# Edge attention on one Trainium2 core: the gathered rows' buffer grows from eight to ten quarters, paid for with spilled tiles and one product buffer less

## The chip, the cores and the metric

The program runs on one core of one Trainium2 chip. The metric is the time of one execution in device microseconds, the median of several runs. The engines are PE (TensorE), DVE (VectorE), ACT (ScalarE), POOL (GpSimd) and SP, which here only issues DMAs.

## What is computed

A graph transformer layer over N = 3125 nodes of width 256 and E = 50000 edges. The part around the change is the attention over edges, whose destinations come sorted:

```
q, k, v = per node, 8 heads of 32
sim  = sum over d of q[dst] * k[src] / sqrt(32)      # per edge and head
p    = exp(sim - max of sim over the edges with this dst)
agg  = segment_sum(p * v[src], dst) / segment_sum(p, dst)
x    = x + agg @ Wo.T + bo + linear attention(x)
x    = x + mixture of 8 experts (layernorm(x))
```

## The kernel before

The layer runs as five blocks, one after the other, with all engines meeting between them: preparation (projections, edge tables), linear attention, edge attention, `finish` (output projection, routing) and `experts`. The change lies in `attention`.

Edge attention walks over CH = 28 chunks of U = 16 steps. A step is 128 edges, one per partition, that lie in one window of 125 destination nodes; the last chunk has only 8 real steps. For each step POOL issues one gather (L965): an indirect DMA that fetches, for 128 edges, a row of 520 words (the key and, per head, the value and a one) from `kv_d` in DRAM. Before each of them a small POOL copy (L955) makes an index column ready eight steps ahead. Four steps are a quarter ("quad"); a chunk has QUADS = 4 of them, so a quarter holds four gathers of 266 KB.

The rows lie in two tiles, `slot0` for even chunks and `slot1` for odd ones, so in eight quarters. A quarter is read twice by DVE: by `product` (L1058, query times key, as soon as the gathers of the quarter have landed: semaphore `arrived`) and, one to two rounds later, by `weigh` (L1074, weight times value, `pv_made`). A gather into a quarter therefore waits until the `weigh` of the same quarter two chunks earlier has been done (L963).

Engines run in rounds; round n works on three chunks at a time. The order on DVE in round n, with c = n - 1 and b = n - 2, is written out by hand: weigh(b,2), an add, product(n,0), an add, local maxima of c, reduce(n,0), carries of c, weigh(b,3), adds, maxima of c, product and reduce(n,1), weigh(c,0), product(n,2), reduce(n,2), rescale, weigh(c,1), adds, `turned_hots` (L1052) for chunk n+1, product and reduce(n,3). `turned_hots` reads `locrow`, which SP loads for each chunk with one 500 KB DMA (L941) as soon as the last `turned_hots` is over. PE spreads the queries (L1197) and sums the weighted values (L1207, which waits for `hot` of ACT, `pv` of DVE and the last add). ACT builds `hot` for a quarter (L992 four Abs, L996 one Relu).

POOL begins the block with 17 tiles of an addition (L648) and eight index copies, and then issues the gathers of chunks 2 to 27 without anything else between them; chunks 0 and 1 were gathered in the block before. `rounds` (L918) emits rounds 0 and 1, a loop of 12 passes over two rounds each, and four more rounds.

After the attention, `finish` multiplies with `woT` on PE (L1488) and adds the product to `base`, the residual tiles (L1385).

Of the kernel before, what the change touches and what calls it, by code (L numbers as in the profile page):

```python
# [25 lines left out]
H, HD = 8, 32  # L26
# [28 lines left out]
SOON = 8  # L55
EARLY = U * KV - NT * (2 * HID + 1)
assert EROWS * W2 >= E and EROWS % 2 == 0 and PAIRS % 2 == 0 and REST == U // 2 and CH % 2 == 0 and CAP == 489
# [83 lines left out]
def prepare(nc, m, io):  # L141
# [3 lines left out]
    with ExitStack() as ctx:  # L145
# [7 lines left out]
        qr = sb("q_rest", [TT, 2, D])  # L153
        qm = sb("qm", [TT, NT, MH])
        sq = sb("sq", [TT, 2, D])
# [49 lines left out]
        with nc.Block() as block:  # L205
# [114 lines left out]
            def _(dve):  # L320
# [37 lines left out]
                def rows_numbered():  # L358
# [5 lines left out]
                    st.then(dve.tensor_scalar(away[:, :], step_no[:, :], U - 0.5, float(NOBODY), ALU.is_ge, ALU.mult))  # L364
# [286 lines left out]
def linear_attention(nc, m, io):  # L651

    with ExitStack() as ctx:
# [19 lines left out]
        ysq = sb("ysq", [TT, 2, D])  # L673
# [187 lines left out]
def attention(nc, m):  # L861
# [7 lines left out]
    with ExitStack() as ctx:  # L869
# [5 lines left out]
        slot, locrow = [m.slot0, m.slot1], m.locrow  # L875
        hotT = sb("hotT", [TT, U, 128], BF16)
        prod = sb("prod", [128, 2, 4, D])
# [15 lines left out]
        habs = sb("habs", [128, 4, TT])  # L893
# [41 lines left out]
        with nc.Block() as block:  # L935
            @block.sync
            def _(sp):
                def body(n, par, turn):
                    if exists(n) and not (isinstance(n, int) and n == 0):
                        wait(sp, S.hotT_made, n)  # L940
                        sp.dma_start(locrow[:, :], loc_c[bass.ds(n, 1), :].to_broadcast([TT, U * 128])).then_inc(S.loc_in, 16)  # L941
                rounds(sp, body)

            @block.gpsimd
            def _(pool):
# [8 lines left out]
                def index(c, par, u):  # L954
                    pool.tensor_copy(m.idx[:, par, u:u + 1], at(m.src_e, c)[:, u:u + 1]).then_inc(S.idx_ready, 1)  # L955

                def gather(c, par, steps):
                    for u in range(steps):
                        if u % 4 == 0:
# [3 lines left out]
                            pool.wait_ge(S.pv_made, QUADS * c + u // 4 + 1 - 2 * QUADS)  # L963
                            pool.nop(nofuse=True)
                        pool.indirect_dma_start(slot[par][:, u, :], None, m.kv_d,  # L965
                                                bass.IndirectOffsetOnAxis(ap=m.idx[:, par, u:u + 1].bitcast(U32), axis=0),
                                                bounds_check=N - 1, oob_is_err=False).then_inc(S.arrived[par * QUADS + u // 4], 16)
                        if u + 8 < steps:
                            index(c, par, u + 8)
                        elif steps == U:  # L970
                            index(c + 1, 1 - par, u + 8 - U)
                for u in range(8):
                    index(2, 0, u)
                with pool.Fori(1, CH // 2 - 1) as k:
                    gather(2 * k, 0, U)
                    gather(2 * k + 1, 1, U)
                gather(CH - 2, 0, U)
                gather(CH - 1, 1, U - REST)

            @block.scalar  # L980
            def _(act):
# [6 lines left out]
                def hots(c, g):  # L988

                    wait(act, S.hot_made, QUADS * c + g)  # L990
                    for u in range(4 * g, 4 * g + 4):
                        last = act.activation(habs[:, u % 4, :], m.iota_w[:, :], ACT.Abs, bias=at(m.nloc_e, c)[:, u:u + 1])  # L992
                    last.then_inc(S.hot_abs, 1)
                    act.wait_ge(S.hot_abs, QUADS * c + g + 1)
                    wait(act, S.summed, PC * c + 2 * g - 2)
                    act.activation(hot[:, 4 * (g % 2):4 * (g % 2) + 4, :], habs[:, :, :], ACT.Relu, bias=m.one_col[:, 0:1],  # L996
# [24 lines left out]
                def body(n, par, turn):  # L1021
# [25 lines left out]
            def _(dve):  # L1047
# [6 lines left out]
                def product(n, par, turn, q):  # L1054
                    dve.wait_ge(S.arrived[par * QUADS + q], 64 * turn + 64)
                    dve.wait_ge(S.q_spread, QUADS * n + q + 1)
                    wait(dve, S.reduced, QUADS * n + q - 1)
# [812 lines left out]
```

## Time and profile before

| | |
|---|---|
| median of 3 runs | 1229.21 us (1227.22 to 1231.34) |
| the profiled execution, its own time | 1221.9 us |
| its span in the profile | 1220.2 us |
| DVE busy over the span | 71% |
| POOL busy over the span | 56% |
| PE busy over the span | 77% |
| the attention block | about 204 to 908.5 us |

The profile is that of one execution. Busy shares are means over blocks with different limits, so what is said on the attention is read from that block alone: from who waits for whom there, and from the timeline of single engines. In a timeline the number in brackets is how long the engine had been idle, and whose work ended that.

### The profile page before, as it was taken

How to read it: one execution, taken by the hardware profiler on the slowest of the kernel's cores; microseconds unless marked ns; L12 is line 12 of the kernel's file. 1: busy time of each engine (PE TensorE's matmuls, PEld its weight loads, DVE VectorE, ACT ScalarE, POOL GpSimd, SP SyncE). 2: the span in 40 equal slices, each digit the busy share in tenths (PEclk: the TensorE clock that was granted, in tenths of full speed). 3: DMA queues.
4: the chain of work that ended last, by engine and by line, in shares of the span. 5: the costliest groups of instructions: out<-in, count | busy, mean ns of one | idle time of the engine just before them, and what ended most of it. 6: DMA issues, size and time to landing. Idle time of an engine off the chain costs nothing. (4 is left out here: it accounts for less than half of the span.)

```text
span 1220.2 us, 18503 instructions
## 1 busy us (share of the span) xinstructions
PE 940.9 (77%) x4059; PEld 648.3 (53%) x4060; DVE 867.9 (71%) x1761; ACT 478.9 (39%) x1312; POOL 681.8 (56%) x1043
## 2 busy tenths in 40 slices
PE   4899776676777677787777768776768389999996
PEld 3455453454545455555555545554546246666664
DVE  3778767778888788887888788887968604444333
ACT  3556535434444344533444334443433033222330
POOL 2534276567778777787778877887500212222321
PEclk9999877878889877887788878888889779999998
DMA  4344272366566655566556655555413143233310
GB/s 146 103 103 95 79 225 77 89 175 191 164 175 184 179 166 164 170 175 179 153 169 163 173 153 163 154 158 161 116 46 109 63 142 124 90 111 102 137 59 8
DMA packets 79290, 164.39 MB, mean 135 GB/s; under 512 B 15472, under 2 KB 46963, under 8 KB 79251
## 3 DMA queue, kind: packets, MB, share of 16 engines
q0 software_dynamic: 38464, 110.26, 32.7%
q1 hardware_dynamic: 38883, 52.22, 13.3%
q10 hardware_dynamic: 1904, 1.45, 0.4%
q8 instruction: 16, 0.26, 0.1%
q14 instruction: 23, 0.19, 0.1%
HBM read 162.03 MB, written 17.65 MB: 147 GB/s over the span
## 5 line engine op out<-in xcount | busy, mean ns | idle before, releaser
L965 POOL DMA_INDIRECT slot<-kv_d,idx x408 | 426.6, 1046 | 149.3 <-DVE at_pv L1074 87.5
L1207 PE MATMUL at_pa<-at_pv,at_hot 128*125 128x264 f32 x880 | 288.5, 472 | 135.4 <-DVE agg L1088 133.3
L1207 PEld LDWEIGHTS at_pa<-at_pv,at_hot 128*125 128x125 f32 x880 | 186.7, 229 | 214.1 <-DVE agg L1088 140.2
L1197 PE MATMUL at_pq<-q,at_hotT 125*128 x1320 | 190.0, 306 | 11.1 <-POOL at_sign L951 7.0
L1058 DVE TENSOR_TENSOR at_prod<-at_pq,slot 128x1024 f32<-128x1024 f32 x110 | 134.0, 1218 | 76.6 <-DMA slot<-kv_d,idx 72.0
L1197 PEld LDWEIGHTS at_pq<-q,at_hotT 125*128 125x128 bf16 x1320 | 138.8, 109 | 46.0 <-issue 13.9
L1074 DVE TENSOR_TENSOR at_pv<-slot,at_pp 128x1056 f32<-128x1056 f32 x110 | 136.9, 1244 | 15.0 <-PE at_pp L1230 14.8
L992 ACT ACTIVATE at_habs<-iota_w,nloc_e 128x125 f32<-128x125 f32 x440 | 138.0, 384 | 3.4
L1065 DVE TENSOR_REDUCE at_sc<-at_prod 128x32 f32<-128x1024 f32 x110 | 133.4, 1213 | 2.0
L996 ACT ACTIVATE at_hot<-at_habs,one_col 128x500 f32<-128x500 f32 x110 | 78.3, 712 | 126.0 <-PE at_pa L1207 122.6
L1613 POOL DMA_INDIRECT out<-slot,node_s x32 | 31.9, 997 | 166.9 <-DVE slot L1645 166.0
L1680 PE MATMUL xp<-slot,hm 128*128 128x256 f32 (+1 forms) x512 | 113.1, 379 | 0.0
L1634 DVE TENSOR_TENSOR y<-xp,b 128x256 f32<-128x256 f32 (+1 forms) x32 | 13.6, 424 | 139.3 <-PE xp L1680 139.3
L1670 PE MATMUL xp<-hT,slot 128*128 128x489 f32 x256 | 108.6, 583 | 0.8 <-ACT hT L1578 0.8
L1680 PEld LDWEIGHTS xp<-slot,hm 128*128 128x128 f32 (+1 forms) x512 | 94.3, 185 | 18.2 <-issue 3.5
L1088 DVE TENSOR_TENSOR agg<-agg,at_pa 125x264 f32 x220 | 92.6, 421 | 7.6 <-PE at_pa L1207 2.8
L1027 ACT ACTIVATE at_row<-at_pchain 1x256 f32<-1x256 f32 x28 | 10.5, 376 | 202.9 <-PE at_pchain L1219 202.9
L1589 ACT ACTIVATE hm<-xp,b 128x489 f32<-128x489 f32 x64 | 42.9, 671 | 114.5 <-PE xp L1670 114.5
L955 POOL COPY idx<-src_e 128x1 int32 (+1 forms) x408 | 80.5, 198 | 2.6
L1670 PEld LDWEIGHTS xp<-hT,slot 128*128 128x128 f32 x256 | 49.5, 194 | 55.7 <-issue 49.9
L1224 PE MATMUL at_pchain<-at_one_c,at_line 1*128 1x1 f32 x112 | 25.0, 323 | 45.5 <-DVE at_line L1109 45.5
L629 PE MATMUL pa<-slot,xnT 128*125 128x512 f32 x100 | 51.7, 642 | 4.1 <-DVE vst L436 4.1
(316 smaller groups left out, 1263.7 us busy)
## 6 DMA issues: line engine op xcount, KB each, us to landing
slot<-in_w SPq DMA_DIRECT2D x16, 1024.0 KB, 6.3
locrow<-loc_d SPq DMA_DIRECT2D x28, 500.0 KB
slot<-kv_d,idx POOLq DMA_INDIRECT x408, 3.8
kv_d<-vst SPq DMA_DIRECT2D x25, 128.9 KB
base<-in_x SPq DMA_DIRECT2D x5, 625.0 KB
kv_d<-kst SPq DMA_DIRECT2D x25, 125.0 KB
row_d<-base SPq DMA_DIRECT2D x5, 625.0 KB
out<-base SPq DMA_DIRECT2D x1, 3125.0 KB
```

The lines of the kernel that those rows point to most:

```text
L955: pool.tensor_copy(m.idx[:, par, u:u + 1], at(m.src_e, c)[:, u:u + 1]).then_inc(S.idx_ready, 1)
L965: pool.indirect_dma_start(slot[par][:, u, :], None, m.kv_d, bass.IndirectOffsetOnAxis(ap=m.idx[:, par, u:u + 1].bitcast(U32), axis=0), bou ...
L992: last = act.activation(habs[:, u % 4, :], m.iota_w[:, :], ACT.Abs, bias=at(m.nloc_e, c)[:, u:u + 1])
L996: act.activation(hot[:, 4 * (g % 2):4 * (g % 2) + 4, :], habs[:, :, :], ACT.Relu, bias=m.one_col[:, 0:1], scale=-1.0).then_inc(S.hot_made, 1)
L1058: dve.tensor_tensor(prod[:, q % 2, :, :], pq[q % 2].rearrange("p (i d) -> p i d", i=4), slot[par][:, 4 * q:4 * q + 4, 0:D], ALU.mult).then ...
L1065: dve.tensor_reduce(sc[:, :, 4 * q:4 * q + 4].rearrange("p h i -> p i h"), prod[:, q % 2, :, :].rearrange("p i (h d) -> p i h d", h=H), X, ...
L1074: dve.tensor_tensor(pv[:, 4 * (q % 2):4 * (q % 2) + 4, :, :], slot[par][:, four, D:KV].rearrange("p i (h c) -> p i h c", h=H), spread(ph[: ...
L1088: dve.tensor_tensor(dst, dst, pa[p % 2][:, 0:H * VW].rearrange("p (h c) -> p h c", h=H), ALU.add).then_inc(S.added, 1)
L1197: mm = pe.matmul(pq[q % 2][:, u * D:(u + 1) * D], hotT[:, 4 * q + u, :], at(m.q3, wins[u // 2])[:, part, :], start=(part == 0), stop=(part ...
L1207: mm = pe.matmul(pa[p % 2][:, 0:H * VW], hot[:, u % 8, :], pv[:, u % 8, :, :].rearrange("p h c -> p (h c)"), start=(u % 2 == 0), stop=(u % ...
L1670: mm = pe.matmul(p1[f % 2][:, 0:CAP], w1[par][:, c, f * 128:(f + 1) * 128], hT[par][:, c, 0:CAP], start=(c == 0), stop=(c == 1))
L1680: mm = pe.matmul(p2[i % 2][0:sizes[i], 0:D], hm[:, f, 128 * i:128 * i + sizes[i]], w2[par][:, f, :], start=(f == 0), stop=(f == FC - 1))
```

## The change

The gathered rows lie in a ring of RING = 10 quarters. Quarter q of chunk c lies at place (4c + q) mod 10. Places 0 to 7 are the old tiles, place 8 is the room of the first eight residual tiles of `base`, place 9 is a new tile `extra`. A gather waits for the `weigh` ten quarters back instead of eight. Room comes from:

- SP writes the first eight tiles of `base` (1.02 MB) and `woT` (0.27 MB, which now lies in `extra`) to DRAM at the start of the attention, and loads both again once the last `weigh` is done; `finish` waits for both before its first use of them.
- `prod` has one buffer instead of two, so a product waits for the reduction just before it.
- `habs` is gone: ACT writes the Abs straight into `hot`, and so waits for PE's sums before the four Abs and not before the Relu.
- some tiles of other blocks (`q_rest`, `sq`, `ysq`, `hT`) move into `extra`.

Since 5 chunks are 20 quarters, two turns of the ring, the loop now holds five rounds: three rounds ahead of it, 4 passes over five rounds, seven rounds behind it.

```diff
-            body(0, 0, 0)
-            body(1, 1, 0)
-            with eng.Fori(1, CH // 2 - 1) as k:
-                body(2 * k, 0, k)
-                body(2 * k + 1, 1, k)
-            for n in range(CH - 2, CH + 2):
-                body(n, n % 2, n // 2)
+            for n in range(LOOP):
+                body(n, n, 0)
+            with eng.Fori(0, LOOPS) as k:
+                for s in range(LOOP, LOOP + TURN):
+                    body(TURN * k + s, s, k)
+            for n in range(CH - 5, CH + 2):
+                body(n, n, 0)
...
+                sp.dma_start(m.first_rows.rearrange("p (t d) -> p t d", t=SOON), m.base[:, 0:SOON, :]).then_inc(S.spilled, 16)
+                sp.dma_start(m.wo_d.rearrange("p (c n) -> p c n", c=2), m.woT[:, :, :]).then_inc(S.spilled, 16)
...
+                sp.wait_ge(S.pv_made, QUADS * (CH - 1) + quads(CH - 1))
+                sp.dma_start(m.woT[:, :, :], m.wo_d.rearrange("p (c n) -> p c n", c=2)).then_inc(S.reloaded, 16)
+                sp.dma_start(m.base[:, 0:SOON, :], m.first_rows.rearrange("p (t d) -> p t d", t=SOON)).then_inc(S.reloaded, 16)
...
-                            pool.wait_ge(S.pv_made, QUADS * c + u // 4 + 1 - 2 * QUADS)
+                            if s == 2 and q < 2:
+                                pool.wait_ge(S.spilled, 32)
+                            else:
+                                pool.wait_ge(S.pv_made, QUADS * c + q + 1 - RING)
...
-                    wait(act, S.hot_made, QUADS * c + g)
+                    four = slice(4 * (g % 2), 4 * (g % 2) + 4)
+                    wait(act, S.summed, PC * c + 2 * g - 2)
                     for u in range(4 * g, 4 * g + 4):
-                        last = act.activation(habs[:, u % 4, :], m.iota_w[:, :], ACT.Abs, bias=at(m.nloc_e, c)[:, u:u + 1])
+                        last = act.activation(hot[:, u % 8, :], m.iota_w[:, :], ACT.Abs, bias=at(m.nloc_e, c)[:, u:u + 1])
...
-                    wait(dve, S.reduced, QUADS * n + q - 1)
+                    wait(dve, S.reduced, QUADS * n + q)
...
+                    if t == 0:
+                        dve.wait_ge(S.reloaded, 32)
                     dve.tensor_tensor(m.base[:, t, :], m.base[:, t, :], po[par][:, 0:D], ALU.add).then_inc(S.x2_made, 1)
...
+                pe.wait_ge(S.reloaded, 32)
```

On POOL, at the start of the attention, this is the order before: the additions, the index copies, and then the first gather of chunk 2, already in the loop and behind a wait for a `weigh`.

```order
L648 TENSOR_TENSOR base<-base,agg 125x256 [waits y_scaled] x17
L955 COPY idx<-src_e 128x1 x8
L974 UNCONDITIONAL_BRANCH
L974 ISA
L963 ISA [waits idx_ready]
L965 DMA slot0<-kv_d,idx 128x520 [waits pv_made]
L955 ISA
L955 COPY idx<-src_e 128x1
```

And this is the same place in the changed kernel (`base` and `extra` are the places 8 and 9 of the ring).

```order
L651 TENSOR_TENSOR base<-base,agg 125x256 [waits y_scaled] x17
L971 COPY idx<-src_e 128x1 x8
L986 DMA base<-kv_d,idx 128x520 [waits idx_ready,spilled]
L971 COPY idx<-src_e 128x1
...
L986 DMA extra<-kv_d,idx 128x520 [waits idx_ready,spilled]
L971 COPY idx<-src_e 128x1
...
L986 DMA slot0<-kv_d,idx 128x520 [waits idx_ready,pv_made]
L971 COPY idx<-src_e 128x1
```

Eight gathers now wait for the spill alone, and the ninth is the first that waits for a `weigh`.

On SP, in the attention and at the start of `finish`, this stood before: one `locrow` DMA a round, and then the loads of `finish`.

```order
L941 DMA locrow<-loc_d 125x2048 [waits hotT_made]
L923 UNCONDITIONAL_BRANCH
...
L941 DMA locrow<-loc_d 125x2048 [waits hotT_made] x2
L935 UNCONDITIONAL_BRANCH
L1335 UNCONDITIONAL_BRANCH [waits barrier_Pool_Activation_PE_DVE_SP_release]
L1337 DMA gb<-in_gate_b 125x8
```

Now the spill stands ahead of the first `locrow`, and the reload behind the last (`first_rows_d` and `wo_d` are the new tensors in DRAM).

```order
L947 DMA first_rows_d<-base 125x2048
L948 DMA wo_d<-extra 128x528
L953 DMA locrow<-loc_d 125x2048 [waits hotT_made] x2
L924 UNCONDITIONAL_BRANCH
...
L953 DMA locrow<-loc_d 125x2048 [waits hotT_made] x5
L956 DMA extra<-wo_d 128x528 [waits pv_made]
L957 DMA base<-first_rows_d 125x2048
L944 UNCONDITIONAL_BRANCH
```

Two DMAs are queued ahead of the `locrow` of chunk 1 on SP's queue, and two ahead of the loads of `finish`.

## Rows read from the trace of the kernel before

**Rows 1.** The page's part 1, busy time, share of the span, instructions.

```profile
PE 940.9 (77%) x4059; PEld 648.3 (53%) x4060; DVE 867.9 (71%) x1761; ACT 478.9 (39%) x1312; POOL 681.8 (56%) x1043
```

**Rows 2.** The waits: engine, line, waited for: us in total, times, longest.

```profile
POOL slot L965 <- DVE at_pv L1074: 87.5, 62, 13.8
DVE at_prod L1058 <- DMA slot<-kv_d,idx: 72.0, 25, 5.6
POOL slot L965 <- issue: 57.3, 317, 1.6
...
DVE at_run L1106 <- ACT at_row L1027: 17.3, 18, 1.5
...
DVE at_pv L1074 <- PE at_pp L1230: 14.8, 16, 1.5
```

**Rows 3.** Timeline, POOL's gathers: start, us, instruction, idle before it.

```profile
231.64 1.08 POOL L965 DMA_INDIRECT slot<-kv_d,idx  x1 [13.78 <-DVE at_pv L1074]
...
414.34 1.02 POOL L965 DMA_INDIRECT slot<-kv_d,idx  x1 [1.58 <-issue]
...
588.83 1.02 POOL L965 DMA_INDIRECT slot<-kv_d,idx  x1 [0.42 <-issue]
...
592.96 1.36 POOL L965 DMA_INDIRECT slot<-kv_d,idx  x1 [0.15 <-issue]
...
874.43 1.00 POOL L965 DMA_INDIRECT slot<-kv_d,idx  x1 [0.30 <-issue]
```

**Rows 4.** Timeline of DVE: a table, first products of rounds, the last weigh.

```profile
215.97 1.02 DVE L1052 TENSOR_SCALAR at_hotT<-locrow,iota_p 125x2048 bf16<-125x2048 bf16 x1
...
245.47 1.22 DVE L1058 TENSOR_TENSOR at_prod<-at_pq,slot 128x1024 f32<-128x1024 f32 x1 [5.57 <-DMA slot<-kv_d,idx]
...
576.37 1.22 DVE L1058 TENSOR_TENSOR at_prod<-at_pq,slot 128x1024 f32<-128x1024 f32 x1 [2.53 <-DMA slot<-kv_d,idx]
...
600.74 1.22 DVE L1058 TENSOR_TENSOR at_prod<-at_pq,slot 128x1024 f32<-128x1024 f32 x1 [3.08 <-DMA slot<-kv_d,idx]
...
874.39 1.23 DVE L1058 TENSOR_TENSOR at_prod<-at_pq,slot 128x1024 f32<-128x1024 f32 x1 [0.22 <-issue]
...
903.47 1.25 DVE L1074 TENSOR_TENSOR at_pv<-slot,at_pp 128x1056 f32<-128x1056 f32 x1
```

**Rows 5.** All gathers of L965, from issue to landing.

```profile
DMA to landing us min/median/max: 2.1/3.8/7.1
```

**Rows 6.** Stretches: busy us of each engine, granted clock, DMA share, GB/s.

```profile
205.00:206.00 1.00, 0.07 (x1) 0.07 (x1) 0.00 (x0) 0.93 (x3) 1.00 (x2) 0.50 0.05 20
...
206.00:209.00 3.00, 3.00 (x15) 2.18 (x16) 0.19 (x1) 2.96 (x4) 3.00 (x6) 0.50 0.35 137
...
992.00:994.00 2.00, 2.00 (x7) 0.90 (x6) 0.00 (x0) 0.99 (x2) 0.00 (x0) 1.00 0.34 121
...
370.00:403.00 33.00, 22.29 (x130) 15.82 (x128) 27.69 (x47) 12.80 (x36) 28.48 (x47) 0.97 0.74 207
...
330.00:860.00 530.00, 392.02 (x1899) 281.53 (x1898) 441.26 (x698) 216.18 (x610) 419.09 (x675) 0.83 0.60 167
```

**Rows 7.** Timeline: SP's locrow of chunk 1, PE's first product of `finish`.

```profile
204.96 0.26 SPq L941 DMA_DIRECT2D locrow<-loc_d  x1
...
911.51 0.80 PE L1488 MATMUL opo<-woT,anT 128*125 128x264 f32 x1
```

**Rows 8.** Timeline: ACT's Relu of a quarter in mid-loop, PE's use of it.

```profile
586.54 0.71 ACT L996 ACTIVATE at_hot<-at_habs,one_col 128x500 f32<-128x500 f32 x1 [0.59 <-PE at_pa L1207]
...
592.82 3.14 PEld L1207 LDWEIGHTS at_pa<-at_pv,at_hot 128*125 128x125 f32 x8 [2.23 <-DVE agg L1088]
```

**Rows 9.** The page's part 5 (costliest groups), the four Abs of a quarter.

```profile
L992 ACT ACTIVATE at_habs<-iota_w,nloc_e 128x125 f32<-128x125 f32 x440 | 138.0, 384 | 3.4
```

**Rows 10.** The page's part 3, the queues by which instructions are loaded.

```profile
q8 instruction: 16, 0.26, 0.1%
q14 instruction: 23, 0.19, 0.1%
```

More of the change, by code:

```diff
@@ L952, in _, with index, gather @@
                 add_mixed(pool, m, SOON, NT)
-                def index(c, par, u):
-                    pool.tensor_copy(m.idx[:, par, u:u + 1], at(m.src_e, c)[:, u:u + 1]).then_inc(S.idx_ready, 1)
-                def gather(c, par, steps):
+                def index(c, s, u):
+                    r = place(s, u // 4)
+                    pool.tensor_copy(m.idx[:, r, u % 4:u % 4 + 1], at(m.src_e, c)[:, u:u + 1]).then_inc(S.idx_ready, 1)
+                def gather(c, s, steps):
                     for u in range(steps):
-                        if u % 4 == 0:
+                        q, i = u // 4, u % 4
+                        r = place(s, q)
+                        if i == 0:
@@ L968, in gather @@
                         if u + 8 < steps:
-                            index(c, par, u + 8)
+                            index(c, s, u + 8)
                         elif steps == U:
-                            index(c + 1, 1 - par, u + 8 - U)
+                            index(c + 1, s + 1, u + 8 - U)
                 for u in range(8):
[L973 to L976, printed above, removed]
@@ L977, in _ @@
-                gather(CH - 2, 0, U)
-                gather(CH - 1, 1, U - REST)
+                    index(2, 2, u)
+                gather(2, 2, U)
+                with pool.Fori(0, LOOPS) as k:
+                    for s in range(LOOP, LOOP + TURN):
+                        gather(TURN * k + s, s, U)
+                for c in range(CH - 5, CH - 1):
+                    gather(c, c, U)
+                gather(CH - 1, CH - 1, U - REST)
             @block.scalar
@@ L1143, in body @@
                     if exists(b, 3):
-                        weigh(b, par, 3)
+                        weigh(b, s - 2, 3)
                     if exists(b, 2):
@@ L1154, in body @@
                     if exists(n, 1):
-                        product(n, par, turn, 1)
+                        product(n, s, k, 1)
                         reduce(n, 1)
                     if exists(c, 0):
-                        weigh(c, 1 - par, 0)
+                        weigh(c, s - 1, 0)
                     if exists(b, 3):
@@ L1524, in experts @@
         hb = m.hb
-        hT = [sb(f"hT_{i}", [128, 2, 512]) for i in range(2)]
+        hT = [m.extra[:, i * 1024:(i + 1) * 1024].rearrange("p (c n) -> p c n", c=2) for i in range(2)]
         hm = sb("hm", [128, FC, 512])
@@ L1723, in __init__ @@
          self.tbl_copied, self.flags_clear, self.gate_summed, self.gc_made, self.gate_step, self.gate_sum, self.nmr_made,
-         self.hn_made, self.hits_made, self.parts_known) = (new(n) for n in names)
+         self.hn_made, self.hits_made, self.parts_known, self.spilled, self.reloaded) = (new(n) for n in names)
 class Inputs:
@@ L1801, in graph_layer @@
             m.slot1 = att.enter_context(nc.sbuf_tensor("slot1", [128, U, KV], F32))
+            m.extra = att.enter_context(nc.sbuf_tensor("extra", [128, 4 * KV], F32))
+            m.woT = m.extra[:, 0:2 * (D + EX)].rearrange("p (c n) -> p c n", c=2)
+            m.quads = [s[:, 4 * q:4 * q + 4, :] for s in (m.slot0, m.slot1) for q in range(QUADS)]
+            m.quads += [w.rearrange("p (u c) -> p u c", u=4) for w in (m.wide_base[:, 0:4 * KV], m.extra[:, :])]
             m.locrow = att.enter_context(nc.sbuf_tensor("locrow", [TT, U * 128], BF16))
```

75 lines of the change are left out of this document (41 added, 34 removed).

## The prediction

> **What bounds the kernel now.** I began with the page's busy shares [rows 1]: no engine is full over the span, so the shares decide nothing. The waits say more [rows 2]. POOL's gathers waited 87.5 us for `weigh`, and DVE's products waited 72.0 us for gathered rows to land. The two wait for each other: the gather is late because its quarter is not free, and the product is late because the gather was. To see which of them is slower by itself I read both in the timeline.
>
> *POOL.* From the first gather at 231.64 to the last at 874.43 pass 642.8 us [rows 3]. Of the 87.5 us of waits for `weigh`, 13.78 lie ahead of the first gather; the other 61 waits sum to 73.7 us. An idle stretch of 0.15 us stands ahead of nearly every gather, whether it waits or not [rows 3], so 61 x 0.15 = 9.2 us of these would be there anyway. The ring costs POOL 73.7 - 9.2 = 64.5 us. What is left, 642.8 - 64.5 = 578.3 us for 407 steps, is 1.42 us each or 22.7 us a round of 16. This holds the small extras: 1.36 instead of 1.02 us for the gather beside `turned_hots`, 0.42 instead of 0.15 at a chunk's end, two stalls of 1.58 us [rows 3].
>
> *DVE.* The first product of chunk 2 starts at 245.47, that of chunk 27 at 874.39: 628.9 us for 25 rounds [rows 4], 25.2 us each. Chunk 2's wait of 5.57 us lies ahead of that stretch, so 72.0 - 5.57 = 66.4 us of waits for rows lie in it. Without them it is 562.5 us, 22.5 us a round. A good round is shorter: 576.37 to 600.74 is 24.37 us, less its wait of 3.08 leaves 21.3. The difference are the waits for ACT's row and for PE's transposed weights, 17.3 and 14.8 us in all [rows 2]; the granted clock in the loop is 0.83 on the mean, so a part of PE's work is done at the lower of its two levels [rows 6].
>
> So the attention runs at 25.2 us a round while POOL alone needs 22.7 and DVE with its partners 22.5. The shortage of quarters costs the rest.
>
> **The change, part by part.**
>
> *Ten quarters.* Gather (n,3) used to wait for weigh(n-2,3), which DVE does in round n itself, some 5 us after its first product; now it waits for weigh(n-2,1) of the round before. In the same way every gather gets two quarters, about 11 us, more room. In the steady state POOL must have the last gather of (n+1,0) out 3.8 us, at worst 7.1, ahead of the product [rows 5]; against that the ring now leaves more than 10 us. I take both kinds of waits as gone, up to what the slower party dictates.
>
> *Start.* POOL is through with its index copies at about 218. It then waits for the spill alone, where it waited until 231.64. Eight gathers fit in, 8 x 1.38 = 11.0 us. But the spill delays DVE. SP's `locrow` of chunk 1 was issued at 204.96 [rows 7] and used at 215.97 [rows 4]. DMAs between DRAM and 125 partitions run at a DMA share of a third: 137 GB/s for the `locrow` read and 121 GB/s for a write [rows 6]. First bytes come about 0.8 us after the issue: in the microsecond after 205 the share is still 0.05 [rows 6]. The spill, issued at 204.0 as the block begins, moves its 1.02 MB from about 205.0 in 8.5 us at 121 GB/s; `locrow` (0.5 MB) comes behind it on the same queue, 3.7 us at 137, plus some 0.3 to land: 217.5, against a start of `turned_hots` at 215.97. Cost: 1.5 us. Bounds: 0, if the two share engines better; 3, with `woT` ahead as well.
>
> The Trainium skill (DMA: Bandwidth & Descriptors, "Why a DMA increments its semaphore by 16 and not by 1") says a copy uses the largest number of engines up to 16 that divides its outer dimension, which for 125 is 5. The share of 0.34 agrees with it. By its 27 GiB/s per engine (Specifications) the spill would take an estimated 7.1 us and not 8.5, and the sum would be about 1.8 us better over spill and reload; the row is the lower rate and I keep it.
>
> *The two limits at chunk 27.* DVE: it could start chunk 2 at 245.47 - 5.57 + 1.5 = 241.4 and needs 562.5 us to the first product of chunk 27: 803.9, against 874.39. That is -70.5. POOL: its last gather moves by -64.5 - 11.0 + 1.5 = -74.0. Both within 4 us; the later one counts. I take -70.5. Fewer slow rounds (PE no longer stands still while DVE waits for rows) would help DVE by up to 32 us, but POOL stops that at -74. Where the two limits are this near, each other's unevenness costs something; the 11 us of room should carry most of it.
>
> *Reload.* SP may load only after the last `weigh`, 903.47 + 1.25 = 904.72 [rows 4]. Two issues of 0.26 us, 0.8 to the first byte, an estimated 0.6 for `woT`, then 1.02 MB at 137 GB/s = 7.5, and 0.3 to land: done 9.8 us later, at 914.5 in the old time. PE's first product with `woT` was at 911.51 [rows 7] and now waits for both loads. Cost: 3.0 us. Bounds: 2 and 5, by 0.1 us more or less per step and the write's 121 GB/s. Queued behind that wait are PE's other 24 products, so everything moves; the expert weights are queued behind the reload on SP, with over 60 us to spare.
>
> *One product buffer.* In DVE's order reduce(n,q) always stands ahead of the next product, with other work between, so the added wait is met. 0. With another order it would cost the latency of a DVE instruction per product.
>
> *Abs into `hot`.* The four Abs (4 x 0.38 us less overlap, about 1.3 us [rows 9]) now come after PE's sums. In mid-loop the Relu at 586.54 moves to about 587.9 and PE uses it at 592.82, so 5 us remain [rows 8]. Only in the last rounds is the gap near zero: 0 to 1.3 us, I take 0.5.
>
> *Loop of five rounds.* It is free by the rows: no instruction wait is seen at the end of a pass before, and only 39 instruction loads happened in the whole run [rows 10]. Bounds: 0 and, with 1.58 us (the longest unexplained POOL stall, rows 3) at each of the 3 jumps back, 5 us. I take 1.
>
> Sum: -70.5 + 3.0 + 0.5 + 1 = -66. The profiled execution (its own time 1221.9, span 1220.2) would be at 1156; the median shown is 7.3 us above it, 1229.2, so the forecast is **1163 us**.
>
> **Rivals.**
>
> *The chain of DVE, PE and ACT is slower than I read it.* If all rounds are like the poor ones, 21.3 + 17.3/18 + 14.8/16 = 23.2 us, chunk 27 starts at 241.4 + 25 x 23.2 = 821.4: -53 + 4.5 = -48.5, 1181. With each wait at its longest, 1.5 + 1.5, it is 24.3 a round and 1208. For it: the PE clock is at the low level part of the time. Against: PE's longest idle stretches are those that vanish.
>
> *DMA becomes the bound.* A round moves 16 x 0.266 + 0.5 = 4.8 MB; at 22.7 us that is 210 GB/s, against 167 on the mean now. From 370 to 403, where POOL hardly waited, 207 GB/s ran at a share of 0.74 [rows 6]. If 207 were the ceiling, a round would be 23.2 us: 1181 too. If gathers slowed so that the ring's new room is eaten by landing times, half of the gain is lost, 1197.
>
> *Only the gathers gain.* POOL runs ahead, PE's clock rises, DVE's good round of 21.3 holds everywhere, and the reload hides: -74, 1155; with no delay at the start either, 1153.
>
> *Slower: instruction loading.* The loop body grows from two to five rounds on every engine. If it no longer stays loaded, each round brings at least one load from DRAM on the engine that sets the pace. The nearest prices are 0.22 us (DVE where the loop is left, rows 4) and 1.58 us (rows 3): 27 rounds x 1.58 = 43 us, 1206. It turns the change into a loss only from 66/27 = 2.4 us a round. The Trainium skill (Runtime: NRT & Kernel Launch, "Instruction fetch mechanics") says that a taken branch to a target outside the loaded pages stalls for a DMA fetch, and speaks against a longer body; no stretch before shows such a stall.
>
> *The change does nothing:* some other wait holds the gathers at 25.2 us a round. The 64.5 us of waits are named for `weigh` alone; I see no other.
>
> **How the numbers follow.** Forecast case (1152 to 1176): 0.66. Poor rounds or DMA near its ceiling (1176 to 1200): 0.20. Better than 1152: 0.05. Partial gain above 1200, or none: 0.05. Slower: 0.04, most of it instruction loading. The range for 8 in 10 runs from 1150 to 1186: the forecast case with the limit of POOL below and the first two rivals' plain prices above. Differences under 0.3% can't be told from no change; faster 0.95, same 0.01, slower 0.04.
>
> **What would show it.** POOL's waits for `weigh` fall from 73.7 us to under 15, and DVE's waits for rows from 72.0 to under 30 (POOL is the slower by a little, so some stay). First products of chunks come 22.5 to 22.9 us apart. The first gather starts near 218. `turned_hots` of chunk 1 starts near 217.5. PE's first product with `woT` comes about 10 us after the last `weigh`. The mean DMA rate in the loop rises to about 185 to 190 GB/s from 167. The forecast fails if rounds stay above 23.5 us: then look for PE's clock, for landing times above 7.1 us, or for `issue` stalls once a pass.

## The result and the profile after

The changed kernel took 1167.63 us (median of 4 runs, 1167.0 to 1168.98) where the kernel before took 1228.22 us (4 runs, 1226.45 to 1231.34): a ratio of 0.9506, 95% interval 0.9483 to 0.9528. The profiled execution has an own time of 1167.82 and a span of 1166.1 us at a granted clock of 0.902; before it was 1221.9, 1220.2 and 0.867. So the traces differ by 54.1 us and the medians by 60.6; the sum of the prediction is checked against the 54.1. In all that follows a median is that of all executions, and a ratio compares only those within 1.5% of the fastest of their kernel.

The page of the changed kernel, part 1, and the two instruction queues of part 3 (answers to [rows 1] and [rows 10]):

```profile
PE 906.9 (78%) x4059; PEld 627.4 (54%) x4060; DVE 871.2 (75%) x1761; ACT 484.8 (42%) x1312; POOL 682.6 (59%) x1043
...
q14 instruction: 80, 0.65, 0.2%
q8 instruction: 22, 0.36, 0.1%
```

The work of DVE and POOL is the same as before to 4 us; the span is shorter because they stand still less. There are 102 instruction loads instead of 39. Where they fall matters more: from 330 to 860 us, in the loop, the trace of before has none, while the new one has 58 from 330 to 800 us.

Of its waits (answers to [rows 2]) one row is new, three waits of DVE ahead of `weigh` that nothing in the profile releases:

```profile
DVE at_pv L1097 <- issue: 16.9, 3, 5.7
```

POOL's gathers wait 14.5 us for `weigh` in all, where they waited 87.5. A wait of DVE for gathered rows, 72.0 us before, is not in the list any more.

The timeline of DVE (start, us, instruction, idle before it): the first table behind the spill, first products of chunks 2, 7, 8, 9 and 27, the weigh at a jump back, and the last weigh (answers to [rows 4]):

```profile
223.52 0.80 DVE L1075 TENSOR_SCALAR at_hotT<-locrow,iota_p 125x2048 bf16<-125x2048 bf16 x1 [0.64 <-DMA locrow<-loc_d]
...
247.25 1.22 DVE L1081 TENSOR_TENSOR at_prod<-at_pq,base 128x1024 f32<-128x1024 f32 x1
...
357.09 1.22 DVE L1081 TENSOR_TENSOR at_prod<-at_pq,base 128x1024 f32<-128x1024 f32 x1
...
382.59 1.25 DVE L1097 TENSOR_TENSOR at_pv<-slot,at_pp 128x1056 f32<-128x1056 f32 x1 [5.71 <-issue]
384.10 1.22 DVE L1081 TENSOR_TENSOR at_prod<-at_pq,slot 128x1024 f32<-128x1024 f32 x1
...
407.11 1.23 DVE L1081 TENSOR_TENSOR at_prod<-at_pq,slot 128x1024 f32<-128x1024 f32 x1 [0.20 <-PE at_pq L1220]
...
811.87 1.22 DVE L1081 TENSOR_TENSOR at_prod<-at_pq,base 128x1024 f32<-128x1024 f32 x1
...
841.87 1.25 DVE L1097 TENSOR_TENSOR at_pv<-extra,at_pp 128x1056 f32<-128x1056 f32 x1
```

From chunk 2 to chunk 27 pass 564.6 us, 22.58 a round. The three rounds that hold a jump back take 27.0 to 27.4 us (357.09 to 384.10 is the first); without the 16.9 us of the jumps the mean is 21.9, and most rounds are 21.2 to 22. The round right behind each of these three is long too: 23.0 (384.10 to 407.11), 24.3 and 24.4 us. The other 19 take 21.6 on the mean.

POOL's timeline (answers to [rows 3]) and the landing times of L986 (answer to [rows 5]):

```profile
222.15 1.08 POOL L986 DMA_INDIRECT base<-kv_d,idx  x1 [0.44 <-issue]
...
238.85 1.02 POOL L986 DMA_INDIRECT slot<-kv_d,idx  x1 [5.76 <-DVE at_pv L1097]
...
808.90 0.99 POOL L986 DMA_INDIRECT extra<-kv_d,idx  x1 [0.30 <-issue]
```

```profile
DMA to landing us min/median/max: 2.4/3.8/8.6
```

The stretch in the rounds (busy us of each engine, granted clock, DMA share, GB/s; answer to [rows 6]):

```profile
340.00:800.00 460.00, 347.76 (x1827) 252.45 (x1827) 422.41 (x673) 213.11 (x590) 400.64 (x643) 0.90 0.68 183
```

DVE is busy for 422.41 of 460 us, 92%. The granted clock there rose from 0.83 to 0.90. It is not even within the stretch. Three windows, the first in good rounds, the other two right behind the second jump's wait:

```profile
335.00:357.00 22.00, 16.78 (x107) 12.67 (x104) 21.16 (x35) 11.68 (x32) 19.45 (x31) 1.00 0.68 186
...
497.30:506.00 8.70, 5.18 (x14) 3.64 (x14) 6.84 (x13) 2.40 (x8) 7.06 (x12) 0.51 0.56 155
506.00:523.00 17.00, 14.60 (x65) 10.74 (x66) 15.62 (x23) 7.19 (x21) 12.96 (x22) 0.75 0.62 165
```

PE had gone idle while DVE stood still, and its granted clock fell from 1.00 to 0.51, near the lower of its two levels, and was back at 1.00 only in the next round (523 to 545 us). The long rounds behind the jumps go with this lower clock, so the jumps cost more than the 16.9 us of their waits.

The end, PE's first product with `woT` (answer to [rows 7]; SP had issued the two loads at 843.15 and 843.55), and a stretch of the reload alone (the columns are those of [rows 6]):

```profile
856.43 1.37 PEld L1514 LDWEIGHTS opo<-extra,anT 128*125 128x125 f32 x4 [7.93 <-DMA base<-first_rows_d]
```

```profile
846.00:848.00 2.00, 0.03 (x1) 0.04 (x1) 1.60 (x5) 0.00 (x0) 1.50 (x10) 1.00 0.31 131
```

One thing lies ahead of the change's own work. DVE's small operation on `yss` took 5.25 us instead of 0.76, as long as POOL's eight adds beside it:

```profile
189.43 5.48 POOL L651 TENSOR_TENSOR base<-base,agg 125x256 f32<-125x256 f32 x8
189.69 5.25 DVE L757 TENSOR_SCALAR yss<-yss 125x5 f32<-125x5 f32 x1
```

### The profile page after: what moved, and what is told of

Same layout as the page of the kernel before. It is cut to its first block and busy times, and to the rows that moved or that the text cites. A ratio compares the mean times of both kernels' runs of the same rounds, so it can differ in the third digit from the quotient of the medians.

```text
span 1166.1 us, 17876 instructions
## 1 busy us (share of the span) xinstructions
PE 906.9 (78%) x4059; PEld 627.4 (54%) x4060; DVE 871.2 (75%) x1761; ACT 484.8 (42%) x1312; POOL 682.6 (59%) x1043
## 5 line engine op out<-in xcount | busy, mean ns | idle before, releaser
L986 POOL DMA_INDIRECT slot<-kv_d,idx x320 | 335.6, 1049 | 59.6 <-issue 40.0
L1230 PE MATMUL at_pa<-at_pv,at_hot 128*125 128x264 f32 x880 | 271.3, 452 | 98.2 <-DVE agg L1111 97.2
L1230 PEld LDWEIGHTS at_pa<-at_pv,at_hot 128*125 128x125 f32 x880 | 176.8, 216 | 170.8 <-DVE agg L1111 108.6
L1016 ACT ACTIVATE at_hot<-iota_w,nloc_e 128x125 f32<-128x125 f32 x440 | 139.4, 387 | 141.1 <-PE at_pa L1230 137.6
L1220 PE MATMUL at_pq<-q,at_hotT 125*128 x1320 | 179.4, 295 | 15.9 <-issue 10.2
L1097 DVE TENSOR_TENSOR at_pv<-slot,at_pp 128x1056 f32<-128x1056 f32 x88 | 109.4, 1243 | 18.2 <-issue 16.9
L1081 DVE TENSOR_TENSOR at_prod<-at_pq,slot 128x1024 f32<-128x1024 f32 x88 | 107.3, 1219 | 9.1 <-PE at_pq L1220 8.3
L1696 PE MATMUL xp<-extra,slot 128*128 128x489 f32 x256 | 108.3, 582 | 0.8 <-ACT extra L1604 0.8
L1019 ACT ACTIVATE at_hot<-at_hot,one_col 128x500 f32<-128x500 f32 x110 | 78.3, 712 | 3.6
L1696 PEld LDWEIGHTS xp<-extra,slot 128*128 128x128 f32 x256 | 49.4, 194 | 55.5 <-issue 49.7
```

The lines of the kernel that those rows point to most:

```text
L986: pool.indirect_dma_start(m.quads[r][:, i, :], None, m.kv_d, bass.IndirectOffsetOnAxis(ap=m.idx[:, r, i:i + 1].bitcast(U32), axis=0), boun ...
L1016: last = act.activation(hot[:, u % 8, :], m.iota_w[:, :], ACT.Abs, bias=at(m.nloc_e, c)[:, u:u + 1])
L1019: act.activation(hot[:, four, :], hot[:, four, :], ACT.Relu, bias=m.one_col[:, 0:1], scale=-1.0).then_inc(S.hot_made, 1)
L1081: dve.tensor_tensor(prod[:, :, :], pq[q % 2].rearrange("p (i d) -> p i d", i=4), m.quads[place(s, q)][:, :, 0:D], ALU.mult).then_inc(S.pro ...
L1097: dve.tensor_tensor(pv[:, 4 * (q % 2):4 * (q % 2) + 4, :, :], m.quads[place(s, q)][:, :, D:KV].rearrange("p i (h c) -> p i h c", h=H), spr ...
L1220: mm = pe.matmul(pq[q % 2][:, u * D:(u + 1) * D], hotT[:, 4 * q + u, :], at(m.q3, wins[u // 2])[:, part, :], start=(part == 0), stop=(part ...
```

## The experiments

Theory: the two quarters of lead give the time, and DVE's chain of 21.3 to 22 us a round is now the bound; the longer loop costs 17 us at its three jumps back; spill and reload cost 3 and 6.5 us. "Jump back" is the branch from the end of the loop body to its start, three on each engine here. Rivals: the gain comes from somewhere else in the change, or the new waits of DVE are not the loop's length, or straight code would pay them too.

All runs but e5 fell under other conditions than the result. They form four groups, each with the kernel before beside it: that took 1318.67 us with e1 to e4, 1237.21 with e5, 1284.75 with e6 to e9 and 1314.32 with e10 to e12. Only comparisons inside one group are made; the changed kernel itself ran in the first (e1) and the last (e10). The chip's number doesn't sort them: number 9 shows 1237 and 1314.

**e1 and e10, the changed kernel again**, no edit.

> The changed kernel once more, unchanged. In its first trace one VectorE operation ahead of the rounds (the TENSOR_SCALAR on yss at 189.69 us, 125x5) took 5.25 us instead of 0.76 and moved everything behind it by 4.3 us. If that is chance (which of VectorE and GpSimd came first), this trace shows it short again in at least some executions and the profiled time comes out near 1163.5; if it belongs to the changed kernel (the moved tiles), it is 5.25 us again and the time is 1167 to 1169 again. Either way the three waits of VectorE for nothing but issue at the jumps back of the loop are there, 5.6 to 5.8 us each, and GpSimd's wait for weigh stays under 15 us.

> The changed kernel, unchanged, a third time, with e11 and e12 beside it on one chip. Chips differ: the kernel before took 1228, 1237, 1285 and 1319 us on four of them. Theory: what the change gives hangs on TensorE's granted clock, since with the rows early the round is a chain through VectorE, PE and ScalarE: on a chip where the kernel before takes 1225 to 1240 us (clock near 0.86) the ratio is 0.945 to 0.955, with rounds of 21.3 to 22; where it takes 1270 to 1320 (clock near 0.84, 0.64 to 0.65 ahead of the rounds) the rounds are 25 to 27 and the ratio is 0.975 to 0.995. Rival: the run e1 was an accident of that chip (waits of 9 us that no releaser explains), and the ratio is 0.95 on any other.

Measured: e1 1324.34 us, ratio 0.9943 (0.9872 to 1.0015); e10 1315.6 us, ratio 1.0041 (0.9993 to 1.009). Under these conditions the change gives nothing. e1's expectation failed in the time, with both its cases, and in POOL's waits for `weigh`, 138.7 us instead of under 15; the three waits at the jumps were there (4.7, 5.2 and 5.4 us), and the operation on `yss` was short in both traces, at most 0.57 us. e10's was met in kind, a little above its 0.975 to 0.995. The stretch in the rounds of e1, against 422.41 us of DVE and a clock of 0.90 in the result's trace:

```profile
340.00:800.00 460.00, 315.33 (x1473) 222.25 (x1473) 340.16 (x532) 171.92 (x473) 321.14 (x517) 0.80 0.56 151
```

The clock is lower already ahead of the rounds (0.65 against 0.74 from 150 to 200 us) and in them (0.80), and DVE is busy for 340.16 of 460 us, 74%. From chunk 2's first product at 256.5 to chunk 27's at 962.1 it is 28.2 us a round, 28.3 in e10, above the 25 to 27 expected there. A lower clock is not all: in e1 there are stalls of up to 9 us in which DVE, PE and soon ACT stand idle and POOL goes on. Eight of them stand ahead of a product, 41.8 us in all; one of the two longest, in DVE's timeline:

```profile
662.83 1.23 DVE L1081 TENSOR_TENSOR at_prod<-at_pq,slot 128x1024 f32<-128x1024 f32 x1 [8.98 <-remote]
```

PE had delivered its half of that product (its 24 matmuls into `at_pq` began at 652.39 and took 2.98 us), and POOL had issued its four gathers by 636.3. "remote" means that the profile names no instruction of this core that released it. Not one of e1's or e10's products waited for gathered rows, though POOL's gathers waited 138.7 and 141.9 us for `weigh`: the rows are early there, and POOL waits for DVE's chain.

**e5, the kernel before.** One execution, profiled.

> The kernel before, unchanged, one look. In the runs e1 to e4 the kernel before took 1318.67 us, 90 us more than in the runs that the prediction was made from, and the changed kernel 1324.34 instead of 1167.63: on that chip the change gives nothing that can be told. Theory: that is a property of the chip that those four ran on (waits for issue and a lower granted clock, in both kernels), so this look either gives 1226 to 1232 us again, on a chip like the first, or 1306 to 1327 on a chip like the second, and then its profile shows where the 90 us lie: rounds of 27 to 29 us instead of 25.2, with waits of 6 to 9 us on PE and VectorE that no row of the first trace has. Rival: the kernel's own spread is that wide on any chip; then the time lies between, 1240 to 1300.

Measured: 1228.64 us, and 1237.21 for the other execution of the same kernel beside it. The conditions of the prediction exist still, so neither the first numbers nor e1's are an accident. Its waits are those of [rows 2] (POOL for `weigh` 96.8 us, DVE for rows 75.2), and the operation on `yss` took 0.76 us.

**e2, e6 and e11, the lead taken back.** All of the change stays, but the gathers wait for eight quarters back:

```
-                            else:
-                                pool.wait_ge(S.pv_made, QUADS * c + q + 1 - RING)
+                                pool.nop(nofuse=True)
+                            if QUADS * s + q + 1 > 8:
+                                pool.wait_ge(S.pv_made, QUADS * c + q + 1 - 8)
```

> The changed kernel, all ten quarters in use, but each quarter's gathers wait for the weigh of eight quarters back, as before the change. If the distance of that wait is what gave the time, nearly all of it goes: POOL waits 70 to 95 us for at_pv again, VectorE 55 to 80 us for gathered rows, good and poor rounds alternate as before, and the time is 1225 to 1245 us (the kernel before, plus what the changed kernel pays for spill, reload and jumps back: up to 23 us). Rival: the gain came from where the rows lie, from the single product buffer, or from fewer cycles of the loop; then this is within 10 us of 1167.6.

> As e2, meant for a chip like the first: ten quarters in use, but each quarter's gathers wait for the weigh of eight quarters back. If that distance gave the time: POOL waits 70 to 95 us for at_pv again, VectorE 55 to 80 us for gathered rows, 1225 to 1245 us, 0 to 1.3% over the kernel before. Rival (the gain came from the place of the rows, the one product buffer, or fewer cycles of the loop): within 10 us of 1167.6, a ratio near 0.95.

> The changed kernel with the wait for the weigh of eight quarters back, on the same chip as e10. It holds all costs of the change and not its gain: ratio 1.005 to 1.015 to the kernel before, as in e2 and e6. The difference to e10 is what two quarters of lead give: 60 to 75 us if the chip is like the first, 15 to 45 if it is like the second. Rival (the lead is not what gives the time): no difference to e10.

Measured: 1331.45, 1297.24 and 1330.55 us; ratios 1.0106 (1.0022 to 1.019), 1.01 (1.0036 to 1.0164), 1.0134 (1.0019 to 1.0248). Without the lead the change is a loss of 1% in all three groups, as the theory says (e2's and e6's absolute times were those of the result's conditions, and failed). What comes back is DVE's wait for gathered rows: 16.3 us in e2, 41.3 in e6 and 9.1 in e11, against none in e1 and e10. The largest part of it, in e6:

```profile
DVE at_prod L1082 <- DMA slot<-kv_d,idx: 32.8, 12, 4.1
```

POOL's waits for `weigh` tell the two apart less well here: 161.7, 137.6 and 171.5 us without the lead, 138.7 and 141.9 with it. And what the lead gives is small: 1331.45 - 1324.34 = 7 us between e2 and e1, 1330.55 - 1315.6 = 15 us between e11 and e10, with executions that scatter by 17 to 36 us; by the ratios 1.6% and 0.9%. The 60 to 75 us of the theory could not be tested, since no run with the lead taken back fell under the result's conditions.

**e3 and e7, no loop.** All thirty rounds are written out on every engine (the same is done for POOL's gathers):

```
-            for n in range(LOOP):
-                body(n, n, 0)
-            with eng.Fori(0, LOOPS) as k:
-                for s in range(LOOP, LOOP + TURN):
-                    body(TURN * k + s, s, k)
-            for n in range(CH - 5, CH + 2):
+            for n in range(CH + 2):
                 body(n, n, 0)
```

> The changed kernel with all thirty rounds written out, no loop on any engine and so no jump back. If the three waits of VectorE for issue (5.6 to 5.8 us, 16.9 in all) are the loading of the loop's code after a taken branch, they are gone, and with them what they cost: 14 to 19 us, time 1149 to 1154. Rival 1: straight code has to be loaded too, and VectorE waits for issue in many small pieces; then the time stays at 1160 to 1175. Rival 2: the waits fall into idle time that VectorE would have had anyway (GpSimd's 22.7 us a round bounds); then the gain is under 6 us, time over 1161.

> As e3, meant for a chip like the first: the changed kernel with all rounds written out. If the three waits of VectorE at the jumps back (16.9 us) are the loading of the loop's code: they are gone, the first products are 21.2 to 22 us apart throughout, ratio 0.934 to 0.940 to the kernel before (1147 to 1154 us). Rival 1: straight code has to be loaded as well, the waits are spread, ratio 0.945 to 0.955. Rival 2: GpSimd at 22.7 us a round bounds as soon as the jumps are gone: ratio above 0.945, and VectorE waits for gathered rows.

Measured: e3 1284.47 us, ratio 0.9731 (0.9674 to 0.9789), where e1 has 0.9943: 2.1%, some 28 us (the traces differ by 30, the medians of all executions by 40); e7 1243.0 us, ratio 0.9656 (0.9611 to 0.97). The direction is the theory's. The size is in e3 more than the 15 us of e1's waits at the jumps: the rounds in which e1 stood still for 9 us ahead of a product are gone too (the longest such wait in e3 is 3.1 us). The absolute times that I gave for both were those of the result's conditions and were missed. The instruction queues of e7 made 35 + 48 = 83 loads, 0.96 MB, almost as much as the 1.01 MB of the changed kernel, and no wait of VectorE for issue in the rounds is longer than 2.9 us. So the same amount of code, loaded in straight order, does not bring the stalls of 5 us and more that it brings behind a jump. That it is wholly free is not shown: e7 has 14 waits ahead of `weigh` without a releaser, up to 3.5 us and 39.3 us in all, and e6 beside it only one; what they wait for is open.

**e9, the kernel before with a longer loop.** Ring of eight, nothing of the change but the length of the body, six rounds run four times (POOL's loop likewise):

```
-            with eng.Fori(1, CH // 2 - 1) as k:
-                body(2 * k, 0, k)
-                body(2 * k + 1, 1, k)
+            with eng.Fori(0, 4) as k:
+                for s in range(6):
+                    body(6 * k + 2 + s, s % 2, 3 * k + 1 + s // 2)
```

> The kernel before, ring of eight, with a loop of six rounds run four times in place of two rounds run twelve times: nothing else changed. It isolates what a longer loop body costs: three jumps back, as in the changed kernel. If a jump back costs 5.6 us of VectorE because the body is longer than what stays loaded: three waits of VectorE for issue of 5 to 6 us, and 5 to 17 us more than before (ratio 1.004 to 1.014), less than the sum where GpSimd's lateness covers them. Rival: the waits in the changed kernel have to do with its ring (a semaphore, a register), not with the body's length: no such wait, ratio 0.998 to 1.002.

Measured: 1302.94 us against 1284.75, ratio 1.0124 (1.0085 to 1.0163): 18 us, at the edge of what I expected (5 to 17 us, ratio 1.004 to 1.014). At each of the three jumps back DVE stands still ahead of `weigh` and again right behind it:

```profile
423.62 1.25 DVE L1074 TENSOR_TENSOR at_pv<-slot,at_pp 128x1056 f32<-128x1056 f32 x1 [6.66 <-issue]
427.31 0.43 DVE L1088 TENSOR_TENSOR agg<-agg,at_pa 125x264 f32 x1 [2.43 <-issue]
```

At the three jumps together these waits are 29.7 us; the time is longer by 18 us. POOL's gathers go on meanwhile, so part of a wait can be made up later; how much is not shown. The instruction queues made 85 + 20 = 105 loads, against 39 for the two-round body [rows 10]. This shows that the price comes with the longer body and needs nothing of the ring. The Trainium skill (Runtime: NRT & Kernel Launch, "Instruction fetch mechanics") says that a taken branch whose target is outside the loaded pages stalls for a DMA fetch of the target. The traces agree with that rule: 5.7 us in the changed kernel, 6.7 + 2.4 in e9, nothing in the body of two rounds.

**e4, e8 and e12, spill and reload in two parts.** The first rows of the base tiles go as 112 and 13 partitions, in e8 and e12 on top of e7's edit (shown is the reload; the spill is split alike):

```
-                sp.dma_start(m.base[:, 0:SOON, :], m.first_rows.rearrange("p (t d) -> p t d", t=SOON)).then_inc(S.reloaded, 16)
+                for a, b in ((0, 112), (112, TT)):
+                    sp.dma_start(m.base[a:b, 0:SOON, :], m.first_rows.rearrange("p (t d) -> p t d", t=SOON)[a:b]).then_inc(S.reloaded, 16)
```

> The changed kernel with spill and reload of the residual rows as two transfers each, of 112 and of 13 partitions, in place of one of 125. If the 125 partitions keep the transfer from most of the 16 engines, the first rows go at 170 GB/s or more instead of 121: the first rows are 2 to 4 us shorter at either end, PE's first product with woT comes 8 to 10 us after the last weigh in place of 13.3, and the time falls by 3 to 7 us, to 1161 to 1165. Rival: the rate is not set by the partition count (it is that of DRAM writes and reads in 8 KB rows); then nothing moves, 1166 to 1169.

> e7 with spill and reload of the first rows as transfers of 112 and of 13 partitions instead of 125. If 125 partitions use few of the 16 engines: spill and reload are each 2 to 4 us shorter and the time is 4 to 7 us under e7 (ratio 0.003 to 0.006 lower); PE's first product with woT comes 8 to 10.5 us after the last weigh instead of 13.3. Rival: the partition count changes nothing, same as e7 within 2 us.

> No loop, spill and reload in two transfers each, on the same chip as e10. On a chip like the first: 1137 to 1147 us where e10 has 1167, a ratio of 0.925 to 0.935 to the kernel before (17 us of jumps back, 4 to 7 of spill and reload, less what other waits take back). On a slower chip 0.955 to 0.965, as e8, and 15 to 30 us under e10. Rival: on a fast chip GpSimd's own 22.7 us a round take over once the jumps are gone; then it gains under 12 us on e10 and VectorE waits for gathered rows.

Measured: e4 1314.22 us, ratio 0.9978 (0.9932 to 1.0024), against e1's 0.9943 not to be told apart, though PE's product comes 8.7 us after the last weigh instead of 12.3. e8 1233.25 us, ratio 0.9586 (0.9541 to 0.9632), 9.8 us under e7. e12 1274.72 us, ratio 0.973 (0.9633 to 0.9828), 41 us under e10. From the last weigh's end to PE's first product with `woT` pass 13.5 us in e7 and 7.4 in e8, against 6.8 in the kernel before; in all traces it is 11.5 to 14.1 us undivided and 7.4 to 8.7 in two parts. PE's wait for the reload there falls from 7.4 us in e7 to 0.7 in e8. A microsecond of e8's reload, before the loads of `finish` are issued:

```profile
918.00:919.00 1.00, 0.89 (x5) 0.41 (x3) 0.43 (x1) 0.00 (x0) 0.00 (x0) 1.00 1.04 352
```

The DMA share is 1.04 here (a packet is counted where it starts, so a share can pass 1) and 0.31 in the undivided reload. That also answers a rival that I did not test, that two transfers are faster than one whatever their shapes: two at a share of 0.31 each would not fill all the engines. At the start the table of chunk 1 comes 15.9 us behind the one of chunk 0 in e7 and 13.9 in e8; but DVE waited for PE there in e7 and not for `locrow`, and by the first product of chunk 2 only 1.1 us of the 2.0 are left. So 7 of the 9.8 us are accounted for, where I had expected 4 to 7 in all; the rest lies in the rounds and at the end. e12 made the absolute numbers of its slower case wrong (0.973 instead of 0.955 to 0.965) and its distance to e10 larger (41 instead of 15 to 30).

No loop with two-part transfers is the best version found: it beats the kernel before in both groups in which it ran (e8, e12) and the changed kernel in the one that had it (e12). It did not run under the result's conditions. There 1167.6 - 16.9 - 7.2, some 1143 us, is an estimate from the trace after and from e7 and e8, but too hopeful a one. In that trace POOL issues the last gather of a chunk's first quarter 18.4 us ahead of its product at chunk 19, behind a jump, and only 8.3 us ahead at chunk 27. POOL regains its lead at the jumps; without them its own pace would soon be the bound, as rival 2 of e7 has it. With its 5.6 us of waits in the rounds taken off and a landing time of 3.8 us, chunk 27 could start some 10 us earlier and not 16.9: an estimate of 1150 us.

## Why the prediction was right, and where its sum was off

**The mutual waits.** Right as a mechanism under the conditions it was made for. Behind the first gather that needs one, POOL's waits for `weigh` fell from 73.7 to 8.7 us, and DVE's for rows from 72.0 to nothing (I had said under 15 and under 30). The last gather of a chunk's first quarter now goes out 8.3 us or more ahead of its product, where it was 5.2 to 9.3. That the gain goes when the lead goes is shown in small by e2 against e1 and e11 against e10 (and e6 without the lead is a loss); its full size is read from the two traces alone, and no experiment shows it.

**The two limits at chunk 27.** Predicted -70.5 for DVE; chunk 27's first product moved by 811.87 - 874.39 = -62.5. The 8.0 us between are: 4.3 for the later start of the block, which comes from the `yss` operation and not from the change's steps; about 1.6 more by chunk 2; and 564.6 instead of 562.5 us for the 25 rounds. That last term is right by luck, two errors that cancel: without the jumps' waits the rounds take 21.9 us and not 22.5, for the poor rounds became fewer as PE's clock rose, and the waits cost 16.9. The rival "only the gathers gain" named that rise. POOL's limit was read rightly: from the ninth gather at 238.85 to the last pass 570.1 us, less 5.6 us of waits for `weigh` beyond the usual 0.15 each, for 399 steps, 22.6 us a round against the 22.7 forecast. No product waited for it because of its head start and of the jumps, at which it caught up. The last gather moved by 808.90 - 874.43 = -65.5, not -74.0.

**Start.** First gather predicted near 218, 222.15 is that plus 4.3. The table of chunk 1 came 7.55 us later than in [rows 4], 4.3 upstream and 3.2 from the change: twice the 1.5 taken, a little over the bound of 3. `locrow` landed that late behind the spill, but DVE waited for it only 0.64 us. The rest it would have lost anyway: PE began to spread the queries 3.9 us after the start of chunk 0's table and not 1.9, which no row of mine foresaw. That is so in every trace with the spill in one part (3.4 us in two parts), in none without it, and what PE waits for is not seen. Another 0.5 is the single product buffer: in round 0 nothing stands between a reduction and the next product, and that product starts 1.36 us after the reduction's start instead of 1.14. (I had written that other work always stands between them.)

**Reload.** Predicted 9.8 us from the last weigh to PE's product and a cost of 3.0; measured 856.43 - 843.12 = 13.3 and a cost of 13.3 - 6.8 = 6.5, outside the bounds of 2 to 5. The step that was mis-sized is "0.6 for `woT`, then 1.02 MB at 137 GB/s". `woT` took 1.3 us, and the first rows 10.2 and not 7.5. Their rate was near the forecast at first, 131 GB/s (846 to 848 us). But I had the expert weights "queued behind the reload" at no cost, and they were issued behind it and moved beside it: in the trace one 8 KB packet of the reload takes 0.31 us until the first packet of the weights at 849.3, and 0.56 after. At the first rate the rows would have been there some 2.4 us sooner. e8 shows what the shape costs: with 112 and 13 partitions the same bytes are there 6.1 us sooner, in good part before the weights are issued. The Trainium skill's rule that the prediction weighed (DMA: Bandwidth & Descriptors, "Why a DMA increments its semaphore by 16 and not by 1") should have been read as advice on the change and not only as a rate: by it 125 rows use 5 of 16 engines and 112 use 16. The traces agree, with shares of 0.31 and 1.04.

**Product buffer, Abs into `hot`.** Predicted 0 and 0.5. The buffer cost the 0.5 us in round 0. From chunk 27's first product to the last weigh's end it is 31.25 us against 30.33: 0.9 in the last rounds, as bounded. No run took these edits alone; e6, which holds them with the jumps, spill and reload, loses only 12 us in all, so they can't be dear.

**Loop.** Predicted 1, bounds 0 to 5, from "no instruction wait is seen at the end of a pass before". Measured 16.9 in waits, and 18 us by e9 in another group. With the long rounds behind the jumps, at a lower clock, it is more: the six rounds take 153.3 us where six others take 130, so 23 us. This is the step that failed: in the body of two rounds the trace shows no load at all (330 to 860 us), so it says nothing about a body that does not stay loaded. The rival had the mechanism, but priced it by POOL's 1.58 us and put it in each round; it is 5.7 us, on DVE, once in five.

The sum: -62.5 + 0.9 + 6.5 = -55.1 at PE's product, -54.1 at the end, against -66 predicted. The errors are 15.9 (loop), 3.5 (reload), 1.6 (start), 0.4 (last rounds) and 4.3 (upstream), 25.7 in all; 25 rounds without jumps at 547.7 instead of 562.5 us give 14.8 back, and 1.0 is lost behind PE's product: 11.9, the difference between 66 and 54.1. So the mechanism was right and the size near partly by luck. The median of 1167.6 against 1163 looks nearer still, because the profiled execution of before, 1221.9, lay below all its timed ones (1226.45 to 1231.34).

**What the prediction did not see:** that the gain hangs on the conditions. The rival "the chain of DVE, PE and ACT is slower than I read it" is what e1 and e10 look like, further than its 24.3 us a round. When the chain takes 27 to 28 us by itself, POOL's 22.7 are largely hidden with eight quarters as with ten (DVE waits 16.3 us for rows in e2, 9.1 in e11), and what is left of the change are mostly its costs. Shown: the same kernel has ratios of 0.9506, 0.9943 and 1.0041, with clocks in the rounds of 0.90, 0.80 and 0.81; and without a loop it gains 2.7 to 3.4% even there. Open: what decides the conditions. A lower clock is seen with it, and so are stalls without a releaser, of which those of 9 us go with the loop (e3) and those of 4 us ahead of the scans do not (28.9 us in e1, 48.1 in e3). No run was made to find out.

## What to carry to other kernels

A loop body that shows no load of instructions in its passes can't price a longer one; write the rounds out, or count the instruction queues' packets and the `issue` waits at the jump. A deeper ring gains only the mutual waits that the consumer's own chain does not cover, so the gain shrinks as that chain slows, and it has to be measured under more than one condition. State parked in DRAM goes faster in 112 and 13 partitions than in 125. A transfer queued behind another is not behind it in time: it took bandwidth from the one that was waited for.

## What the runs showed of the hardware that I had not expected

- A jump back over a five-round body stalled VectorE, 5.5 to 5.7 us each, while GpSimd went on issuing; over a six-round body 6.4 to 6.8 and then 2.4 to 4.0 us. Straight code with 83 loads has no wait of VectorE for issue above 2.9 us in the rounds.
- Behind each such stall PE's granted clock was 0.51 to 0.67 for 8 to 9 us and 0.73 to 0.79 for the rest of the round.
- PE's first work behind the spill starts 2.0 us later than without it, in all eight traces with the spill in one part, and no row says for what.
- One and the same kernel, the one before, took 1228 to 1319 us in different groups of runs, with a scatter inside a group of 5 us in the first and 12 to 25 in the others. The kernels without a loop scatter by only 4 to 5 us there.
- A VectorE operation on 125x5 elements took 5.25 us while GpSimd ran eight adds in 5.48; where it took 0.76 (e5) the same eight adds took 6.83. That VectorE is held off by GpSimd is argued from these rows; no run isolates it. The Trainium skill (Trainium Architecture — The Big Picture, "What this means for kernel authors") says that these two engines share a pair of ports under an exclusive lock. The traces agree with that rule and do not prove it.
